# A new order of five instruction queues in the last phase of a two-layer decoder

## The reference, cut to what matters

```
def _L1_xattn_ref(x, ctx, Wq, Wk, Wv, Wo):           # 16 heads of 16
    q = heads(x @ Wq); k = heads(ctx @ Wk); v = heads(ctx @ Wv)
    scores = jnp.einsum('bhqd,bhkd->bhqk', q, k) * scale
    weights = jax.nn.softmax(scores, axis=-1)
    out = jnp.einsum('bhqk,bhkd->bhqd', weights, v)
    return merge(out) @ Wo

def _L1_ffn_ref(x, w_gate, w_up, w_down):
    gate = fp4_linear(x, w_gate); y = fp4_linear(x, w_up)   # both sides quantised in blocks of 16
    h = jax.nn.silu(gate) * y
    return fp4_linear(h, w_down)

x = x + _L1_xattn_ref(_layernorm(x), ctx_768, ...)
x = x + _L1_ffn_ref(_layernorm(x), ...)
```

## Time and profile before

| what | value |
|---|---|
| median of three runs | 3350.12 us (3347.3 to 3352.28) |
| profiled execution | 3352.28 us, its span 3350.5 us |
| busy: TensorE, VectorE, ScalarE, GpSimd | 92%, 69%, 54%, 39% |
| mean granted clock of TensorE | 0.969 of full |

### The profile page before, as it was taken

How to read it: one execution, slowest core, us unless ns; L and a number is a source line. 1 busy time by engine, 2 the same in 40 slices (tenths; PEclk the granted TensorE clock), 3 DMA queues, 4 the chain that set the end, 5 groups by cost and what they waited for, 6 DMA issues and landing times. The chain is left out here.

```text
span 3350.5 us, 57669 instructions
## 1 busy us (share of the span) xinstructions
PE 3097.9 (92%) x21302; PEld 2161.8 (65%) x21302; DVE 2314.2 (69%) x4781; ACT 1792.6 (54%) x3243; POOL 1297.6 (39%) x1933
## 2 busy tenths in 40 slices
PE   3899999999999998699999786899999999999997
PEld 2566666666666665366666554567777777777765
DVE  3588888888888887333111385587888887887784
ACT  3788788888888884111111132355555555455542
POOL 4366666666666653100000252133333333333332
PEclk8899999999999998699999898899999999999999
DMA  5977777877777773332334254433344334433320
GB/s 98 149 122 109 104 110 108 108 109 103 109 104 109 108 101 56 116 109 93 116 118 141 61 166 101 68 60 57 61 71 65 56 57 68 67 62 57 61 44 14
DMA packets 291101, 301.17 MB, mean 90 GB/s; under 512 B 35242, under 2 KB 278426, under 8 KB 290820
## 3 DMA queue, kind: packets, MB, share of 16 engines
q1 hardware_dynamic: 276420, 273.41, 47.4%
q0 software_dynamic: 6144, 15.68, 1.6%
q10 hardware_dynamic: 8256, 8.39, 0.8%
HBM read 95.51 MB, written 50.40 MB: 44 GB/s over the span
## 5 line engine op out<-in xcount | busy, mean ns | idle before, releaser
L493 DVE TENSOR_REDUCE xa_mx<-bank 128x2 f32<-128x512 f32 x1024 | 663.1, 687 | 253.1 <-PE bank L483 248.8
L597 ACT ACTIVATE xa_p<-bank 128x512 f32<-128x512 f32 x1024 | 564.5, 599 | 285.2 <-PE bank L587 282.6
L608 DVE SCALAR_TENSOR_TENSOR xa_p<-xa_p,bank 128x1024 f32<-128x1024 f32 x256 | 306.6, 1217 | 49.0 <-PE bank L576 31.4
L933 POOL TENSOR_SCALAR_AFFINE_SELECT xa_p<-xa_p 128x256 f32<-128x256 f32 x512 | 202.9, 410 | 225.2 <-ACT xa_p L924 212.7
L620 PE MATMUL bank<-xa_p,xa_v 128*32 128x256 f32 x4096 | 278.0, 389 | 1.8 <-DVE xa_p L608 1.6
L924 ACT ACTIVATE xa_p<-bank 128x384 f32<-128x384 f32 x512 | 237.0, 492 | 62.0 <-PE bank L912 43.9
L1952 POOL DMA_INDIRECT sa_y<-expert_out,sa_s x64 | 70.3, 1099 | 510.5 <-POOLq L1853 484.1
L1747 ACT ACTIVATE ex_h<-bank,ex_b 128x512 f32<-128x512 f32 x64 | 44.0, 687 | 362.5 <-PE bank L1736 362.5
L1736 PE MATMUL bank<-ex_xt,ex_w 128*128 128x512 f32 x512 | 225.3, 598 | 0.7 <-ACT ex_xt L1727 0.7
L1766 PE MATMUL bank<-ex_w,ex_h 128*128 128x256 f32 x1024 | 224.0, 379 | 1.0 <-issue 0.9
L1766 PEld LDWEIGHTS bank<-ex_w,ex_h 128*128 128x128 f32 x1024 | 193.4, 190 | 28.1 <-issue 2.4
(11 more groups left out here) (284 smaller groups left out, 6824.8 us busy)
## 6 DMA issues: line engine op xcount, KB each, us to landing
ex_w<-ra_parts SPq DMA_DIRECT2D x384, 128.0 KB, 5.1
xa_ks<-xa_pk SPq DMA_DIRECT2D x384, 128.0 KB, 4.5
ex_w<-in_L_ffn_W SPq DMA_DIRECT2D x32, 1024.0 KB, 7.2
xa_qs<-xa_pq SPq DMA_DIRECT2D x192, 128.0 KB, 4.7
ex_w<-xa_pq SPq DMA_DIRECT2D x192, 128.0 KB, 4.5
ra_x<-in_x SPq DMA_DIRECT2D x32, 256.0 KB
xa_ctx<-in_ctx_t SPq DMA_DIRECT2D x64, 128.0 KB, 2.1
queue<-zeros ACTq DMA_DIRECT2D x4, 2048.0 KB, 8.1
```

Source lines behind the costliest of these rows:

```text
L493: c.nc.vector.tensor_reduce(c.xa.row_max[:, :, n], halves(c.banks[2 + n % 2]), AX.X, ALU.max).then_inc(s.max_taken, 1)
L597: c.nc.scalar.activation(c.xa.p_beside[:, n // 2 % 4, :, n % 2, :], halves(c.banks[n % 2]), ACT.Exp, scale=SCALE).then_inc(s.exp, 1)
L608: c.nc.vector.scalar_tensor_tensor(out=p, in0=p, scalar=1.0, in1=c.banks[bank][:, :].unsqueeze(1).broadcast_to([P, TC, 2 * S]), op0=ALU.mi ...
L933: c.nc.gpsimd.affine_select(out=diagonal, in_=diagonal, compare_op=ALU.is_ge, fill=0.0, base=0, pattern=[[0, TC], [1, P]], channel_multipl ...
```

## The change

All five tables of phase E are written anew; the instructions, their operands and their waits are the same, and every queue has as many as before. The rounds keep their length. One head of the diff and one hunk stand for the rest:

```
@@ def pe_phase_e(c):
-        for b, k in due(n, period, (924, 925, 927, 928, 932, 933, 935, 936, 940, 941, 944, 946, 949, 951, 953, 954)):
+        for b, k in due(n, period, (922, 926, 927, 928, 929, 930, 932, 933, 935, 936, 938, 940, 943, 945, 947, 950)):
             pe_xa_score(c, B + b, k)
...
-        for b, k in due(n, period, (1094, 1096, 1097)):
+        for b, k in due(n, period, (1094, 1095, 1097)):
             pe_e_turn_hidden(c, 2 + k % 2, b, k)
-        for b, _ in due(n, period, (1100,)):
+        for b, _ in due(n, period, (1099,)):
             pe_e_down(c, 7, b)
@@ def dve_phase_e(c):
-        for b, _ in due(n, period, (556,)):
+        for b, _ in due(n, period, (557,)):
             dve_e_quantise(c, b)
-        for b, _ in due(n, period, (588,)):
+        for b, _ in due(n, period, (587,)):
             dve_e_out(c, 7, b)
@@ def sp_phase_e(c, d):
-        for b, _ in due(n, period, (11,)):
+        for b, _ in due(n, period, (12,)):
             sp_xa_stack_q(c, B + b)
-        for b, _ in due(n, period, (18,)):
+        for b, _ in due(n, period, (16,)):
             sp_xa_max_rows(c, B + b)
```

More of the change, by code:

```diff
@@ L2353, in pe_phase_e @@
     period = ROUND_E["pe"]
-    for n in range((B - 1) * period + 1101):
-        for b, _ in due(n, period, (821,)):
+    for n in range((B - 1) * period + 1100):
+        for b, _ in due(n, period, (818,)):
             pe_xa_keys(c, 7, c.wx, B + b)
-        for b, _ in due(n, period, (841,)):
+        for b, _ in due(n, period, (846,)):
+            pe_xa_values(c, 7, c.wx, B + b)
+        for b, _ in due(n, period, (852,)):
             pe_xa_turn(c, 6, B + b)
-        for b, _ in due(n, period, (845,)):
+        for b, _ in due(n, period, (856,)):
             pe_xa_queries(c, 6, c.wx, B + b)
-        for b, _ in due(n, period, (859,)):
-            pe_xa_values(c, 7, c.wx, B + b)
-        for b, k in due(n, period, (871, 872, 880, 881, 885, 887, 890, 892, 897, 898, 901, 904, 905, 909, 911, 912)):
+        for b, k in due(n, period, (881, 884, 888, 891, 893, 895, 896, 898, 900, 901, 903, 905, 907, 909, 911, 913)):
             pe_xa_max(c, B + b, k)
-        for b, _ in due(n, period, (916,)):
+        for b, _ in due(n, period, (917,)):
             pe_xa_turn_rows(c, 2, 1, B + b)
-        for b, k in due(n, period, (924, 925, 927, 928, 932, 933, 935, 936, 940, 941, 944, 946, 949, 951, 953, 954)):
+        for b, k in due(n, period, (922, 926, 927, 928, 929, 930, 932, 933, 935, 936, 938, 940, 943, 945, 947, 950)):
             pe_xa_score(c, B + b, k)
-        for b, k in due(n, period, (934, 942, 952, 960)):
+        for b, k in due(n, period, (931, 937, 944, 955)):
             pe_xa_sum(c, c.xa.s.exp, 16 * (B + b) + 4 * k + 4, B + b, k)
-        for b, _ in due(n, period, (947,)):
+        for b, _ in due(n, period, (948,)):
             pe_xa_turn_sums(c, B + b, 0)
@@ L2374, in pe_phase_e @@
             pe_xa_turn_sums(c, B + b, 1)
[L2375 removed]
+        for b, _ in due(n, period, (970,)):
             pe_xa_turn_out(c, B + b)
[L2377 removed]
+        for b, _ in due(n, period, (976,)):
             pe_xa_project(c, 6, c.wx, B + b)
[L2379 removed]
+        for b, _ in due(n, period, (999,)):
             pe_e_turn(c, 6, b)
[L2381 removed]
+        for b, k in due(n, period, (1010, 1015, 1018, 1024)):
             pe_e_gate(c, b, k)
[L2383 removed]
+        for b, k in due(n, period, (1031, 1032, 1035, 1040)):
             pe_e_up(c, b, k)
[L2385 removed]
+        for b, k in due(n, period, (1094, 1095, 1097)):
             pe_e_turn_hidden(c, 2 + k % 2, b, k)
[L2387 removed]
+        for b, _ in due(n, period, (1099,)):
             pe_e_down(c, 7, b)
@@ L2392, in dve_phase_e @@
     period = ROUND_E["dve"]
-    for n in range((B - 1) * period + 589):
-        for b, _ in due(n, period, (422,)):
+    for n in range((B - 1) * period + 588):
+        for b, _ in due(n, period, (423,)):
             dve_xa_stats(c, c.ff.x[b % 4], c.ff.s.x_in[b % 4], 16 * (b // 4 + 1), B + b)
-        for b, _ in due(n, period, (442,)):
+        for b, _ in due(n, period, (439,)):
+            dve_xa_rest_k(c, 7, c.wx, B + b)
+        for b, _ in due(n, period, (446,)):
             dve_xa_normed(c, c.ff.x[b % 4], B + b)
-        for b, _ in due(n, period, (443,)):
-            dve_xa_rest_k(c, 7, c.wx, B + b)
-        for b, _ in due(n, period, (450,)):
+        for b, _ in due(n, period, (455,)):
             dve_xa_rest_q(c, 6, c.wx, B + b)
-        for b, k in due(n, period, (465, 466, 467, 468, 469, 470, 471, 472, 475, 476, 477, 479, 482, 483, 485, 486)):
+        for b, k in due(n, period, (465, 466, 467, 468, 469, 471, 472, 473, 475, 476, 478, 479, 481, 482, 483, 484)):
             dve_xa_max(c, B + b, k)
-        for b, _ in due(n, period, (509,)):
+        for b, _ in due(n, period, (505,)):
             dve_xa_normalise(c, B + b, 0)
@@ L2407, in dve_phase_e @@
             dve_xa_normalise(c, B + b, 1)
-        for b, _ in due(n, period, (518,)):
+        for b, _ in due(n, period, (519,)):
             dve_xa_add(c, 6, c.ff.x[b % 4], c.ff.x5[b % 4], B + b)
-        for b, _ in due(n, period, (519,)):
+        for b, _ in due(n, period, (522,)):
             dve_e_stats(c, b)
-        for b, _ in due(n, period, (522,)):
+        for b, _ in due(n, period, (524,)):
             dve_e_normed(c, b)
-        for b, k in due(n, period, (551, 552, 554, 555)):
+        for b, k in due(n, period, (549, 551, 552, 554)):
             dve_e_hidden(c, b, k)
-        for b, _ in due(n, period, (556,)):
+        for b, _ in due(n, period, (557,)):
             dve_e_quantise(c, b)
-        for b, _ in due(n, period, (588,)):
+        for b, _ in due(n, period, (587,)):
             dve_e_out(c, 7, b)
@@ L2458, in pool_phase_e @@
         for b, _ in due(n, period, (0,)):
+            pool_xa_low_k(c, B + b)
+        for b, _ in due(n, period, (1,)):
             pool_xa_power(c, B + b)
-        for b, _ in due(n, period, (1,)):
-            pool_xa_low_k(c, B + b)
-        for b, _ in due(n, period, (2,)):
+        for b, _ in due(n, period, (3,)):
             pool_xa_low_q(c, B + b)
-        for b, _ in due(n, period, (10,)):
+        for b, _ in due(n, period, (9,)):
             pool_xa_split_max(c, B + b)
@@ L2476, in sp_phase_e @@
     period = ROUND_E["sp"]
-    for n in range((B - 1) * period + 41):
+    for n in range((B - 1) * period + 42):
         for b, _ in due(n, period, (1,)):
@@ L2483, in sp_phase_e @@
             sp_xa_stack_k(c, B + b)
-        for b, _ in due(n, period, (11,)):
+        for b, _ in due(n, period, (12,)):
             sp_xa_stack_q(c, B + b)
-        for b, _ in due(n, period, (18,)):
+        for b, _ in due(n, period, (16,)):
             sp_xa_max_rows(c, B + b)
-        for b, _ in due(n, period, (40,)):
+        for b, _ in due(n, period, (41,)):
             sp_e_out(c, out_rows[b], b)
```

26 lines of the change are left out of this document (13 added, 13 removed).

## The result

| what | before | after |
|---|---|---|
| median | 3349.4 us (3347.3 to 3352.28, 4 runs) | 3378.87 us (3376.28 to 3380.84, 4 runs) |
| profiled execution, span | 3352.28, 3350.5 us | 3377.66, 3375.9 us |
| a full round | 37.69 us | 38.56 us |

A forecast was written before the change was run, and what follows sets the result against it. TensorE was taken as the bound, 92% busy, with 37.16 of 37.69 us a round being work. 3352.28 + 25.7 (27 rounds at +0.95) - 9 (fill) + 9 (drain) = 3378.0, or 3375.8 against the median; forecast 3375, range 3350 to 3391.

The forecast's parts named there:

- The row of scores: Behind "down", which ends at T, five scores wait on exps; sum at T + 2.47, loss 1.28 us a round.
- A: Rival: the two banks suffice and no score waits; each round wins 0.33 us, total 3341, faster; chance 9%.
- The third turn: Ahead of "down", the third turn meets the first one's bank too early: loss 0.20 us a round.
- The gain of 0.53: Each round, the 0.49 us wait ahead of "down" and 0.04 from the old order of scores 4 and 5 go.
- Row maxima, quantise, SiLU: In a full round, row maxima and quantise cost 0, or 0.3 and 0.5 uncovered; first SiLU has 0.3 us slack.
- rival C: Rival: a second engine falls behind the new order, SiLU or copies slipping 0.5 a round: +13, 3388 us; chance 16%.
- The fill, -9: Start of the phase: earlier row maxima and keys win more than scores in a row lose: -9 us, bounds -14 and +3.
- the walk: Step-by-step estimate of the fill's four rounds: -3.5, -3.3, -1.6 and -0.8 us.
- The drain, +9: Last rounds: quantise waits uncovered for "down" and the output addition, +7.2 in the last; +9 us in all, bounds +4 and +12.
- +3 and -1: Drain rounds before the last: turns of sample 30 wait for its quantise, about +3 us; wins elsewhere, -1.
- The total of 3378.0: Whole kernel on the profiled execution's scale: 3352.28 + 25.7 - 9 + 9 us; 3375.8 against the median.

The follow-up runs named there:

- Experiment 1: Kernel before, with only two maxima and the turn of the quantised input moved out from between the scores behind "down": ratio 1.0081, rounds of 38.57 us.
- experiment 7: Kernel before, with up pieces between the turns, one score ahead of "down", maxima and a turn between scores, row maxima issued earlier for two samples: ratio 1.0112.
- experiment 6: Kernel after, with VectorE's quantise put back ahead of the output addition in every round: 3592.03 us in one run, rounds of 46.62 us.
- Experiment 5: Kernel after, with VectorE's quantise ahead of the output addition for the last samples only: 3377.74 us, ratio 1.0066.

## Why the prediction was right

**The row of scores, 1.28 a round: right, and shown.** The sum was forecast at T + 2.47 and stands at T + 2.48; scores 3 and 5 were forecast at T + 1.08 and T + 2.16 and stand at T + 1.07 and T + 2.15. Experiment 1 makes the loss on the kernel before, and the halved exp changes the new order's round by 0.41 and the old one's by 0.04. That settles the cause against the rival that the two banks suffice (A). The advice of the Trainium skill to rotate banks (Perfetto Trace Analysis, section Matmuls) is followed here and is not enough. From a score's start to the next use of its bank 1.08 must pass (0.42 to the exp, 0.60, 0.06). The order before had 1.31 of work in that time, two scores and the filler (3203.91 to 3205.22 in the earlier trace rows); the row has two scores, 0.44, and exps that follow one another at 0.49 where scores follow at 0.22.

**The third turn, 0.20: right.** It starts 0.41 behind the score (3174.09 to 3174.50), whose work is 0.22: 0.19. Having waited, it takes 0.50 to the next start (3174.50 to 3175.00), where 0.44 was counted.

**The gain of 0.53: a little small.** ScalarE's copies no longer delay "down". What I had not counted is that "down" itself gets shorter: 5.18 from start to start (3176.18 to 3181.36) where the earlier trace rows gave 5.29. In experiment 1 it waits (0.29) and takes 5.28; in experiment 7 it doesn't and takes 5.18. So a waited-for "down" pays 0.1 beyond the wait. I had read 5.29 as pure work. 1.28 + 0.20 - 0.53 = 0.95 was forecast, less 0.11 gives 0.84, 0.87 was measured: 23.5 instead of 25.7 over 27 rounds. The 0.03 left is less than the 0.06 that the third turn took too long.

**Row maxima, quantise, SiLU, each costed at 0 in a full round: right.** No wait on any of them stands in the round after, so rival C (+13) did not occur. That the quantise needs its new place is shown by experiment 6.

**The fill, -9: right in sign, 2.5 too much, and 3.2 if the 0.7 of the phase's earlier start is left out.** The first scores came 5.3 earlier than 2115.07 (3.5 in the walk), the next 8.3 (2139.55 against 2147.80), those of sample 2 9.9 (2172.74 against 2182.68). Of the 9.9, 1.2 is the up piece that now follows score 0 instead of preceding it; the other 8.7 compare with the 8.4 that the walk had there. That nearness is luck in part: the first step was 1.8 better than forecast (0.7 of it the start of the phase), the third 1.2 worse. Then the last round lost 2.2 (6.5 remain at the first "down") where I had it gain 0.8. TensorE there:

```profile
2172.74 0.38 PE L587 MATMUL bank<-ex_w,xa_ks 99*128 99x256 bf16 x2 [0.71 <-DVE ex_w L2296]
...
2174.93 0.61 PE L587 MATMUL bank<-ex_w,xa_ks 99*128 99x256 bf16 x4 [0.62 <-DVE ex_w L2296]
...
2188.86 0.39 PE L483 MATMUL bank<-xa_ks,ex_w 96*128 96x256 bf16 x2 [2.07 <-DVE xa_mx L493]
```

The scores wait for VectorE's products of the first sample, and a maximum for 2.07 while VectorE runs the first quantise (2179.35 to 2188.20 in the trace), as the maxima stand behind it and no "down" is there to cover it. In the kernel before the same quantise starts 0.64 ahead of these scores (2182.68), here 6.61 behind them:

```profile
2182.04 1.62 DVE L1528 TENSOR_REDUCE fp_s<-ex_w 128x88 f32<-128x1408 f32 x1
```

The kernel before has one wait of 0.21 on maxima in that round. This is read from the traces; no experiment took it away. The mis-sized step is the last of the walk: -0.8, where +2.2 stood.

**The drain, +9: right, +8.4.** The last turns start 20.0 behind the second last "down" (20.2 forecast):

```profile
3326.76 0.65 PE L304 MATMUL bank<-ident,fe_xq 128*128 128x128 f32 x4 [2.54 <-POOL fe_xq L1553]
...
3341.98 5.34 PE L454 MATMUL bank<-ff_wd,fe_ht 128*128 128x256 f32 x24
3361.98 2.92 PE L304 MATMUL bank<-ident,ex_w 128*128 128x128 f32 x12 [14.66 <-POOL ex_w L1553]
```

Experiment 5 shows that most of it comes from the quantise behind the addition. I had named one cause for the last round; there are two (5.2 and 1.8). From the 28th "down" to the last one the drain grew by 9.4; the last "down" and what follows took 10.3 in place of 11.2, as that "down" ran at a granted clock of 0.76 in place of 0.67, which I had not forecast.

For the rounds before the last I had +3 and -1 and got +2.4, but the 3 for a reason that did not hold. I had the turns of sample 30 wait for their quantise. They wait 0.66 in the trace, and experiment 5, which quantises earlier there, makes that round no shorter (23.53 against 23.10). What the trace shows in the round that grew from 20.10 to 23.10 is the first row above: the turn of the quantised input starts 7.88 behind its "down" (3318.88), before it was 5.28 (3302.53 to 3307.81), since VectorE's steps on that input now stand behind the product of the last up piece (3319.08). The four gate pieces behind it then run at a granted clock of 0.74 and take 6.48 instead of 4 x 1.19 = 4.76. That term met its number by luck; no run tests the reading.

The total of 3378.0 on the profiled scale met 3377.66, closer than its terms, and that is luck: the fill was 2.5 short of its gain, and the rounds and the drain 2.8 better.

## What to carry to other kernels

When work is reordered, look at what the moved pieces were standing between: two banks hide an evacuation only if, from a group's start to the next use of its bank, the producer has work for the whole way to the end of the evacuation (0.44 here, where 1.08 was needed), and if the whole stretch runs at that pace, a filler moved within it gains nothing. Read the loss from start distances against work, not from idle brackets (0.67 was printed where 1.29 was lost). Check each reordering in the fill and the drain by itself, since cover that a neighbour gives in a full round is missing there; and the tables of several queues are coupled, so that one piece put back alone cost 213 us, by one run, where the whole change cost 27 (experiment 6).

## What the runs showed of the hardware that was not expected

TensorE's clock fell to its lower level in the middle of a busy phase: after a gap of 5.5 us in each round the next 3.45 us ran at a granted clock of 0.54, and the following 7 us at 1.00 again, with 1.00 before the gap (experiment 6). One wait of 0.9 us in each round shows no such thing: the 27 rounds of experiment 7 stand at 1.00. But short waits close together were followed by the lower level too. In the last round of the fill of the kernel after, TensorE waits 0.71, 0.62, 0.47 and 0.20 within 4.7 us, at full clock, and the next 4.8 us run at 0.65:

```profile
2172.74:2177.41 4.67, 3.28 (x17) 1.43 (x17) 3.82 (x13) 2.65 (x5) 0.69 (x1) 1.00 1.06 142
2177.41:2182.22 4.81, 4.81 (x29) 3.05 (x29) 4.64 (x7) 1.79 (x4) 2.33 (x2) 0.65 0.65 112
```

A float32 group that starts right behind another matmul takes 0.1 less from start to start than the same group after a wait (5.18 in the kernels after and of experiment 7, against 5.28 in that of experiment 1 and 5.29 before). What makes the 0.1 no run here tells.
